# Attention's value sums: normalised in blocks of 32 by VectorE, with spread output weights, in place of turns on TensorE

## The reference

```python
h, dqk = 8, 64; dv = 16                      # 8 heads
q, k = split(x @ W_qk); v = x @ W_v          # per head: 64, 64 and 16 wide
dots = einsum('bhid,bhjd->bhij', q, k) * SCALE
attn = softmax(dots + bias[None], axis=-1)   # bias by distance, clipped at 10
out = einsum('bhij,bhjd->bhid', attn, v)
out = out.transpose(0, 2, 1, 3).reshape(b, n, h * dv)
return out @ W_out + b_out
```

## Time and profile before

| | |
|---|---|
| median of 3 runs | 1193.36 us (1192.32 to 1194.19) |
| the profiled execution | 1196.92 us, its span 1195.2 us |
| TensorE busy | 1059.1 us (89% of the span) |
| VectorE busy | 909.4 us (76%) |
| ScalarE busy | 839.0 us (70%) |
| GpSimd busy | 540.7 us (45%) |

### The profile page before, as it was taken

The page is one execution under the profiler, slowest core; times in us unless marked ns, Lnnn a source line. Parts: engine busy times, 40 slices in busy tenths (PEclk is TensorE's granted clock), DMA queues, the critical chain, the costliest instruction groups (busy, mean ns, idle before and its releaser), DMA issues. The chain is left out here.

```text
span 1195.2 us, 23244 instructions
## 1 busy us (share of the span) xinstructions
PE 1059.1 (89%) x7684; PEld 776.8 (65%) x7684; DVE 909.4 (76%) x1962; ACT 839.0 (70%) x1736; POOL 540.7 (45%) x363
## 2 busy tenths in 40 slices
PE   4876599988888889889969999999999999997897
PEld 3432488888878878759964455545455555546897
DVE  7797999989889899747646686868686868675465
ACT  4996899988888899546635666757575757562565
POOL 0389789999999999734530001010101010011354
PEclk9997599999999999999989999999999999998999
DMA  3000344444675574233321000000000000001331
GB/s 94 4 2 28 86 125 127 117 119 128 177 215 148 146 211 135 69 99 104 98 74 45 1 1 19 2 19 1 19 2 19 1 19 6 14 19 59 98 99 52
DMA packets 84437, 83.67 MB, mean 70 GB/s; under 512 B 23735, under 2 KB 62396, under 8 KB 84320
## 3 DMA queue, kind: packets, MB, share of 16 engines
q1 hardware_dynamic: 75440, 60.20, 18.5%
q0 software_dynamic: 5568, 12.66, 3.0%
q10 hardware_dynamic: 3312, 9.33, 2.5%
HBM read 65.73 MB, written 17.35 MB: 70 GB/s over the span
## 5 line engine op out<-in xcount | busy, mean ns | idle before, releaser
L1028 DVE TENSOR_TENSOR_SCAN h<-d_a,p_dbu 128x1024 f32<-128x1024 f32 x128 | 288.8, 2277 | 27.3 <-ACT d_a L794 15.2
L738 POOL TENSOR_TENSOR h<-h,c_rep 128x1024 f32<-128x1024 f32 x126 | 294.4, 2368 | 13.1 <-DVE h L1028 10.9
L1999 ACT ACTIVATE arena<-arena,at_min 128x512 f32<-128x512 f32 x256 | 183.1, 720 | 97.0 <-DVE at_min L2109 93.4
L2109 DVE CUSTOM_DVE_ANT_0 arena<-at_p_scores,arena 128x512 f32<-128x512 f32 x256 | 174.3, 684 | 58.6 <-PE at_p_scores L1867 49.7
L1346 POOL TENSOR_SCALAR r_row<-r_row 128x4 f32<-128x4 f32 x15 | 3.5, 234 | 444.8 <-DVEq L1252 444.8
L794 ACT ACTIVATE d_a<-arena,a_exp 128x511 f32<-128x511 f32 x256 | 169.6, 712 | 22.4 <-DVE h L1028 22.4
L1874 PEld LDWEIGHTS at_p_probs_T<-ident,arena 128*128 128x128 f32 x1024 | 112.2, 141 | 92.4 <-issue 65.3
L786 ACT ACTIVATE b_du_T<-arena,b_T 128x256 f32<-128x256 f32 x392 | 166.3, 498 | 0.0
L1867 PE MATMUL at_p_scores<-arena,at_q_T 64*128 64x512 f32 x512 | 159.3, 641 | 1.5 <-DVE arena L2097 1.5
L1874 PE MATMUL at_p_probs_T<-ident,arena 128*128 128x128 f32 x1024 | 157.0, 281 | 3.4 <-ACT arena L1999 1.6
L918 PE MATMUL p_y_T<-ident,h 128*128 128x128 f32 x1024 | 133.9, 274 | 4.7 <-POOL h L738 4.3
(11 more groups left out here) (258 smaller groups left out, 1651.0 us busy)
## 6 DMA issues: line engine op xcount, KB each, us to landing
c_rep<-c_rows SPq DMA_DIRECT2D x128, 256.0 KB
f_row<-expert_rows SPq DMA_DIRECT2D x78, 129.0 KB, 2.0
diag_b<-diag_rows SPq DMA_DIRECT2D x30, 256.0 KB, 4.1
arena<-in_w_all ACTq DMA_DIRECT2D x8, 578.0 KB
arena<-bias_by_distance ACTq DMA_DIRECT2D x8, 448.0 KB
x_tok<-in_x SPq DMA_DIRECT2D x4, 512.0 KB, 5.8
x_tok<-x_between SPq DMA_DIRECT2D x8, 256.0 KB, 2.6
diag_rows<-diag_b SPq DMA_DIRECT2D x4, 256.0 KB, 3.0
```

The costliest lines, as they stand in the source:

```text
L738: nc.gpsimd.tensor_tensor(h[:, n % HS, :, :], h[:, n % HS, :, :], cc, ALU.mult).then_inc(prod_done, 1)
L1028: nc.vector.tensor_tensor_scan(h[:, n % HS, :, :].rearrange("p c t -> p (c t)"), da[:, s % 2, :, :].rearrange("p c t -> p (c t)"), p_dbu[: ...
L1999: nc.scalar.activation(pr[:, slot, :], sc[:, slot, :], ACT.Exp, scale=-1.0, bias=mn[:, slot:slot + 1]).then_inc(probs_ready, 1)
L2109: V.tensor_tensor_reduce(sc[:, slot, :], psc[:, s % SCB, :], band[:, hd, w0:w0 + T], 1.0, 3.0e38, ALU.add, ALU.min, mn[:, slot:slot + 1]). ...
```

## The change

The value sums stay in blocks of 32. Per group there are four steps, all on VectorE (`norm`): part 0 transposes the PSUM bank `at_p_o_T` in blocks of 32x32 into `o_tok`, so that within each block tokens lie on partitions and a head's 32 rows along it; part 1 takes the reciprocal of the denominators (element 16 of each block); part 2 multiplies all 32 elements of each block; part 3 transposes back in blocks of 32x32 into `onT[gr]`. `NORM_AT` places the parts: group 0 in slots 23, 24, 25 and 27 of its own core, group 1 in slots 3 to 6 of the next. The output weights are spread to match: `w_o` has two groups of 128 rows with 16 rows of each head at 32 q and zeros between, written by GpSimd and loaded by 8 small transfers in place of one. The output product is now 8 products (4 token tiles x 2 groups) in slot `O_AT = 7`. ScalarE's `o_out` and its copy, TensorE's `turn_back` and the turn of slot 7 are gone.

```diff
-        self.w_qk, self.w_v, self.w_o, self.b_o = k.take(2 * H * DQK), k.take(D), k.take(D), k.take(D)
+        self.w_qk, self.w_v, self.w_o, self.b_o = k.take(2 * H * DQK), k.take(D), k.take(2, D), k.take(D)
...
-        sp.wait_ge(self.w_in, 64)
+        sp.wait_ge(self.filled, 3)
+        for hd in range(H):
+            gr, q = hd // 4, hd % 4
+            sp.dma_start(self.w_o[32 * q:32 * q + DV, gr, :], self.k.dram["w_o"][hd * DV:(hd + 1) * DV, :]
+                         ).then_inc(self.w_in, 16)
+        sp.wait_ge(self.w_in, 16 * (3 + H))
...
+        G.memset(self.w_o.rearrange("p g d -> p (g d)"), 0.0).then_inc(self.filled, 1)
...
-            IDLE_BEFORE = {5: 3, 7: 3, 9: 3, 14: 14, 15: 3}
+            IDLE_BEFORE = {O_AT: 9, 14: 14, 15: 3}
...
-                elif s in (3, 5):
-                    turn_back(b, s // 2 - 1)
-                elif s == 7:
-                    mm_there(1, b, 1)
-                    mm_free(0, b, 0)
-                    for j in range(TPB):
-                        mm = nc.tensor.transpose(pmm[:, 0, j * P:(j + 1) * P], on[:, j, :], k.ident[:])
-                    mm.then_inc(mm_done[0], 1)
-                elif s == 9:
-                    mm_there(0, b, 0)
+                elif s == O_AT:
+                    pe.wait_ge(normed, b * NG)
                     mm_free(1, b, O_USE)
                     for j in range(TPB):
-                        mm = nc.tensor.matmul(pmm[:, 1, j * P:(j + 1) * P], onT[:, j * P:(j + 1) * P], w_o,
-                                              start=True, stop=True)
+                        for gr in range(NG):
+                            mm = nc.tensor.matmul(pmm[:, 1, j * P:(j + 1) * P], onT[gr][:, j * P:(j + 1) * P],
+                                                  w_o[:, gr, :], start=gr == 0, stop=gr == NG - 1)
                     mm.then_inc(mm_done[1], 1)
...
-            def o_out(b, gr):
-                act.wait_ge(valued, 1 + b * SV + (gr + 1) * (SV // NG))
-                if not (isinstance(b, int) and b == 0):
-                    act.wait_ge(mm_done[1], use(1, b, gr))
-                copy(oT[gr], pot[:]).then_inc(oT_ready, 1)
...
+            NORM_AT = ((23, 24, 25, 27), (3, 4, 5, 6))
...
+            def norm(b, gr, part):
+                n = b * NG + gr
+                if part == 0:
+                    dve.wait_ge(valued, 1 + b * SV + (gr + 1) * (SV // NG))
+                    dve.wait_ge(norm_step, 2 * n)
+                    V.transpose(o_tok.rearrange("p n e -> p (n e)"), pot[:]).then_inc(oT_ready, 1)
+                elif part == 1:
+                    dve.wait_ge(oT_ready, 1 + n + 1)
+                    V.reciprocal(rden[:], o_tok[:, :, DV]).then_inc(norm_step, 1)
+                elif part == 2:
+                    dve.wait_ge(norm_step, 2 * n + 1)
+                    dve.wait_ge(normed, n)
+                    V.tensor_tensor(o_normed[:], o_tok, rden[:].unsqueeze(2).to_broadcast([P, T // 32, 32]),
+                                    ALU.mult).then_inc(norm_step, 1)
+                else:
+                    dve.wait_ge(norm_step, 2 * n + 2)
+                    if b > 0:
+                        dve.wait_ge(mm_done[1], use(1, b, O_USE))
+                    V.transpose(onT[gr], o_normed[:].rearrange("p n e -> p (n e)")).then_inc(normed, 1)
```

More of the change, by code:

```diff
@@ L1654, in sync @@
     def sync(self, sp):
-        for dst, src in ((self.w_qk, "w_qk"), (self.w_v, "w_v"), (self.w_o, "w_o"), (self.b_o, "b_o")):
+        for dst, src in ((self.w_qk, "w_qk"), (self.w_v, "w_v"), (self.b_o, "b_o")):
             sp.dma_start(dst, self.k.dram[src]).then_inc(self.w_in, 16)
-        sp.wait_ge(self.w_in, 64)
+        sp.wait_ge(self.filled, 3)
[4 more added lines that the diff above has]
+        sp.wait_ge(self.w_in, 16 * (3 + H))
     def flip(self, pe, first, last):
@@ L1712, in attention @@
         k.arena_free, k.arena_end = E_N * WROW, WORDS_B * FREE_FOR_WEIGHTS
-        xl, on, xlT, oT, router_xlT = k.take(TPB, D), k.take(TPB, D), k.take(T), k.take(T), k.take(T)
-        onT = oT
+        xl, xlT, router_xlT, onT0, o_tok = k.take(TPB, D), k.take(T), k.take(T), k.take(T), k.take(T // 32, 32)
         k.arena_free, k.arena_end = at.arena_free, ARENA
-        oT = [oT, k.take(T)]
+        onT = [onT0, sb("o_norm_T", [P, T])[:]]
+        o_normed = sb("o_normed", [P, T // 32, 32])
         qT = [sb(f"q_T{i}", [P, H // 2, T]) for i in range(2)]
@@ L1721, in attention @@
         prT = sb("probs_T", [P, 2, HG, TPB, 2 * P])
-        rden = sb("r_den", [P, TPB, HG])
+        rden = sb("r_den", [P, T // 32])
         SCB = 3
@@ L1744, in attention @@
         valued, oT_ready = S("valued"), S("oT_ready")
-        inverted = S("inverted")
-        HEAD, TAIL = (6, 4), (1, 3)
+        norm_step, normed = S("norm_step"), S("normed")
+        HEAD, TAIL = (6, 4), (0, 1)
         LATE = 26
+        O_AT = 7
         def use(slot, b, u):
@@ L1815, in x_turn @@
                 pe.wait_ge(xl_ready, b + 2)
-                mm_free(0, b, 1)
+                mm_free(0, b, X_USE)
                 for j in range(TPB):
@@ L1821, in project @@
             def project(b, slot, u, m):
-                mm_there(0, b, 1)
+                mm_there(0, b, X_USE)
                 mm_free(slot, b, u)
@@ L1983, in head @@
                 if s == 18:
-                    arrived(b, 1)
+                    arrived(b, X_USE)
                     copy(xlT, pmm[:, 0, :]).then_inc(mm_taken[0], 1)
@@ L2018, in tail @@
                     take(b - 1, ST - 1)
-                elif s == 3:
-                    o_out(b - 1, 1)
-                elif s == 8:
-                    arrived(b, 0)
-                    copy(onT, pmm[:, 0, :]).then_inc(mm_taken[0], 1)
                 elif s == 15:
@@ L2132, in tail @@
                     take(b - 1, ST - 2)
-                elif s in (4, 6):
-                    norm(b, s // 2 - 2)
-                elif s == 10:
+                elif s in NORM_AT[1]:
+                    norm(b - 1, 1, NORM_AT[1].index(s))
+                if s == 10:
                     arrived(b, O_USE)
@@ L2153, in core @@
                         head(-1, 0, s + LATE)
+                    if s in NORM_AT[0]:
+                        norm(b, 0, NORM_AT[0].index(s))
                     if not last:
```

26 lines of the change are left out of this document (5 added, 21 removed).

## The result

| | before | changed |
|---|---|---|
| median of 4 runs, us | 1193.78 (1192.32 to 1195.28) | 1210.88 (1208.44 to 1211.49) |
| the profiled execution, us | 1196.92, span 1195.2 | 1211.07, span 1209.1 |

The ratio is 1.0118, with a 95% interval from 1.0093 to 1.0144: 14.1 us more, between 11.1 and 17.2. I had forecast 15.1 us more, and 1208.5.

What follows compares the result with a forecast made beforehand. TensorE, busy 49.68 of 50 us, was taken to set the pace. Lateness of 14.5 (group 1) plus 1.4 (group 0) less 0.8 (end) gave 15.1 us more: 1208.5 by the median, range 1204 to 1214, wider range 1198 to 1219.

Steps and rivals of the forecast that it cites:

- The mechanism: Group 1's first transpose, ahead of bias(4), makes VectorE stand still 2.46 us for value sums; the slot 4 score pair breaks.
- the walk: Step-by-step clock of core 2's VectorE and TensorE lists after the change, each 128x512 operation taking 0.61 us of queue.
- Slot 10: In group 1's chain, slot 10's scores start at 764.1 in place of 762.46: 1.6 us late.
- The core: Cores 1 to 6 each 2.2 us late, TensorE's 0.44 included; period near 58.7 in place of 56.5.
- The last core and group 0: Last core 1.3 us late from group 1; group 0's wait in slot 23 costs 0.7 over seven cores, 0.7 in the last.
- The end: After the last core, from sums to addition, the chain takes 4.6 us in place of 5.41: gain 0.8.
- TensorE: Turn-backs go, output product doubles: 0.44 us less a core, 3.5 over 8; busy share falls some 3 points.
- The price of a transpose: One 128x512 transpose on VectorE taken as 0.69 us, like a PSUM copy; bounds 0.292 and 1.222.
- the third: Rival: the VectorE transpose is slow, 1.22 us, so 25 us more in all, or 1218; chance 0.15.
- the fourth rival: Only the waits' order is right, transposes cheap at 0.29 us: 11 us more, or 1204; chance 0.1.
- The sum: Whole program: 14.5 for group 1 plus 1.4 for group 0 less 0.8 at the end, 15.1 us more.
- The first rival: VectorE's slack takes all the added work; TensorE's 3.5 and the end's 0.8 are gained: 1189.1; chance 0.12.

Runs made afterwards that it cites:

- wait_only: The kernel before plus one VectorE wait in slot 3 for group 1's value sums, nothing else: 57.33 us a core, ratio 1.0047.
- no_middle: Changed kernel, group 1's parts in slots 4 to 7, product in slot 9, without reciprocal and multiplication of both groups: 56.93 us a core, ratio 1.0012.
- o_at_9: The changed kernel with only the output product moved, from slot 7 to slot 9: 58.88 us a core, ratio 1.0131.
- loads_only: The kernel before plus the change's zero fill and 8 small weight loads, into an unused buffer: 56.50 us a core, ratio 0.9994.
- wait_g0: The kernel before plus one VectorE wait in slot 23 for group 0's value sums: 56.50 us a core, ratio 0.9997.
- spread_stats: Changed kernel, group 1's parts in slots 5, 7, 7, 8, group 0's from 24, product in 9, next statistics in 3, 9, 11, 15: 56.57 us a core, ratio 1.0015.
- double_first: The changed kernel with group 1's first transpose made twice: cores of 58.98 to 58.99 and 60.55 to 60.56 us, ratio 1.0163.

## Why the prediction was right, and which terms were off

- **The mechanism.** All rows it named are there: the transpose starts after 2.38 us of standing still (2.46 forecast), released by the value sums; the second of the pair in slot 4 waits for the bias pass; bias(4) is done about 2.1 us after the sums are there (760.76 against 758.66), as the walk had it (754.93 against 752.82). wait_only shows that the wait alone costs (0.83 a core), no_middle that VectorE's work between bias passes does (0.51 for the two middle parts).
- **Slot 10.** Forecast 1.6 late, measured 1.35. The mis-sized terms stand ahead of bias(5): after bias(4) the reciprocal takes 0.15 of VectorE's queue (0.28 in the walk) and the aggregation 0.24 (0.3), and ahead of it the statistics take 0.74 (0.8). So turn(5) comes 4.45 us after the sums are there (763.11), not 4.68, and the output product starts after 6.49, not 6.78. The product is also mis-sized, 1.78 from 765.15 to 766.93 and not twice 0.97, but that did not count: from its start to slot 10's scores the walk has 4.5 us and the trace 4.50.
- **The core.** Forecast 2.2 late and a period of 58.7, measured 1.97 at slot 12 and 58.38. Six cores: 11.3 in place of 13.2. The last step, cover taken from slots 10 to 12, was put at 0.6 (2.2 less 1.6) and measures 0.62, and o_at_9 bears the reason out: with the product back in slot 9 these slots take what they took before. What the prediction did not say is that the product covers more where it is, in slot 7, and that moving it back would not help.
- **The last core and group 0.** From the first sums of the last core to its last, 45.89 us against 45.81, where I had forecast 2.0 more. But the execution of before stood still once there: the turns issued at 1071.14 were copied out from 1073.62, 2.48 us later, in loads_only 0.70 later (1073.87 to 1074.57). loads_only, with the same code in this stage, took 44.10 from sums to sums, and wait_g0 45.09. So the term lies between 0.1 and 1.8, and one execution of each kernel does not settle it. In the full cores group 0 costs nothing: from slot 12 to the next sums it is 43.51 us, before 43.60 (0.1 forecast), and wait_g0 says the same.
- **The end.** -0.8 forecast, -0.78 measured.
- **TensorE.** 2.5 points less busy, 3 forecast. The price of a transpose, taken from the nearest copy as 0.69, is 0.717 and 0.707. That settles the third and the fourth rival. The Trainium skill ("Vector Engine (DVE) Microarchitecture Reference", The reshape front-end and per-opcode configuration) says that the 32x32 array of the transpose sustains one element per cycle and lane; the trace agrees, since a transpose costs what a copy of as many elements does. Four times the 311 ns that the prediction cited would have been 1.24 us.
- **The sum.** From the stage's first fetch of x to its last addition it is 479.28 us against 468.32, 11.0 more: 0.4 in the first core (loads_only, with before's code there, has 0.3 as well), 11.3 in six, 0.1 to the last sums, less 0.8. The two spans differ by 13.9; the stage starts 3.56 later in the changed kernel's trace, and after it 0.6 comes back. The later start is not the change's. 2.73 us of it are there when GpSimd begins to fill V's constants (529.03 against 526.30), ahead of anything that the change adds. At VectorE's operation at 541.51 (before 537.97) it is 3.54, and the first of the new loads is issued only at 605.32; the 0.8 in between has its like in wait_only, without the change's zeros (0.95). In the 14 profiled executions of this study the stage started between 617.85 and 621.78 us, at 617.85 in double_first, which has the change's zeros and loads. So my 15.1 is nearer to the ratio's 14.1 than its terms deserve, and that is luck. The stage's 11.0 lies at the lower end of the ratio's interval; whether the other 3 us are the change's or what varies outside of the stage, no run shows.
- **The first rival** turned on one point: bias(4) done a microsecond earlier. In spread_stats it is, and still nothing is gained, so that rival's 4.3 us of gain was not to be had by this point alone. The 0.44 us of TensorE is the difference of 1.3 us spared in slots 3 to 8 and 0.89 added with the product. Both places stand in the trace of spread_stats: not all of the first arrives, since turns there wait for exponentials, and the second is paid in full. I read this from the rows; no run removes these waits.

## What to carry to other kernels

An engine that runs its list in order and feeds another one must not wait for something that is not there yet: look up when the input is complete, and place the operation behind the consumer's next need. Here 2.4 us of standing still on an engine that was 24% idle cost 0.8 us a core, and with the four parts one slot early behind it 1.4. Work taken off the full engine counts only in a stretch where that engine sets the pace: some 1.3 us of turns went where it waited for bias passes anyway, and 0.89 us of product came where nothing covered it. Before work is moved off a full engine onto an idle one, look through the receiving engine's waits in the order of its list; the one that was already there, slot 31's copy, was worth more (1.01 us a core) than the change could have been (0.44 of TensorE's work).

## What the runs showed of the hardware

- The transpose of 128x512 in 32 bits takes 717 ns from PSUM and 707 ns (701 into the other buffer) from SBUF, as long as a copy or a product with a broadcast operand (688).
- A period can have two lengths with one and the same order: the granted clock fell to 0.50 for about 3 us in two cores of double_first (60.56 and 60.55 us) and not in the others (58.98). In the stretch before the fall TensorE was busy for 1.38 of 2 us in short pieces, and none of its waits there was longer than 1.54 us. The same waits stand in cores 2, 4 and 6 without a fall, so that they bring it about is not shown.
- The start of the attention stage moved by up to 4 us (617.85 to 621.78) between the nine executions with the change's earlier code, while a core's period repeated to 0.01 us within each, but for double_first. For such a change the period in the trace is a finer measure than the time of the program.
